# Two products fewer on TensorE, and a bias loaded ahead of its weight, in the opening of a conditioned feed-forward kernel

## What is computed

```python
q_emb = relu(cond @ W3 + b3)                       # one row of 512 per batch
h     = (64 * x + x.sum(axis=1, keepdims=True)) * q_emb[:, None, :]
h0    = relu(h @ W2 + b2)
y     = square(relu(h0 @ ternary(W_fc).T))
out   = x + rms_norm(y) @ ternary(W_proj).T
```

## Time and profile before

| | before |
|---|---|
| median of 3 executions | 312.59 us (312.39 to 313.21) |
| the profiled execution's own time | 312.75 us |
| its span, first to last instruction | 311.0 us |
| TensorE busy | 305.5 us, 98% |
| VectorE, ScalarE, GpSimd busy | 61%, 61%, 33% |

### The profile page before, as it was taken

The page is one execution under the profiler, slowest core; times in us unless marked ns, Lnnn a source line. Parts: engine busy times, 40 slices in busy tenths (PEclk is TensorE's granted clock), DMA queues, the critical chain, the costliest instruction groups (busy, mean ns, idle before and its releaser), DMA issues.

```text
span 311.0 us, 3798 instructions
## 1 busy us (share of the span) xinstructions
PE 305.5 (98%) x1286; PEld 233.7 (75%) x1286; DVE 188.7 (61%) x318; ACT 191.1 (61%) x282; POOL 102.0 (33%) x94
## 2 busy tenths in 40 slices
PE   8999999999999999999999999999999999999995
PEld 7764545446888888888888888888888888888883
DVE  0589999995778877888348235952223484222245
ACT  1685366696999699977646554445555445555540
POOL 1012333345433223344342431253333314333330
PEclk9999999999999999999999999999999999999999
DMA  6999435443464041115004300340000033000003
GB/s 211 354 274 277 173 73 99 133 112 93 125 212 103 1 102 37 34 34 52 17 0 147 125 0 1 133 140 0 0 2 0 0 135 137 0 0 0 2 2 136
DMA packets 31332, 27.03 MB, mean 87 GB/s; under 512 B 18736, under 2 KB 20816, under 8 KB 31312
## 3 DMA queue, kind: packets, MB, share of 16 engines
q1 hardware_dynamic: 29936, 26.22, 29.8%
q10 hardware_dynamic: 1376, 0.56, 0.7%
HBM read 18.39 MB, written 4.19 MB: 73 GB/s over the span
## 4 chain that ended last, share of the span: by engine, by line
PE 98%; DVE 0%; issue 0%; POOL 0%; POOLq 0%; DVEq 0%
PE ps_out L360 37%; PE ps_acc L348 37%; PE ps_acc L332 18%; PE ps_out L310 2%; PE ps_out L319 1%; PE ps_acc L404 1%; PE ps_x L419 1%; PE ps_acc L411 0%; PE ps_x L394 0%; DVE x_sb L565 0%; DVE x_t L495 0%; PE ps_x L400 0%; PE ps_acc L407 0%; POOL ident_f L712 0%; POOL ident_f L710 0%
## 5 line engine op out<-in xcount | busy, mean ns | idle before, releaser
L243 POOL TENSOR_TENSOR wv_sb<-wv_sb 128x512 f32<-128x512 f32 x55 | 71.7, 1304 | 122.7 <-DVE y_lo L510 115.6
L348 PE MATMUL ps_acc<-h_hi,w_t 128*128 128x512 f32 x256 | 100.0, 391 | 0.0
L360 PE MATMUL ps_out<-w_t,y_hi 128*128 128x512 f32 x256 | 100.0, 391 | 0.0
L360 PE MATMUL ps_out<-w_t,y_lo 128*128 128x512 f32 x256 | 99.6, 389 | 0.0
L348 PE MATMUL ps_acc<-h_lo,w_t 128*128 128x512 f32 x256 | 99.6, 389 | 0.0
L508 DVE CAST y_hi<-x_t 128x512 fp32r<-128x512 f32 x64 | 33.2, 518 | 86.9 <-PE ps_out L360 70.2
L655 ACT ACTIVATE x_t<-ps_acc 128x512 f32<-128x512 f32 x64 | 37.8, 591 | 61.1 <-PE ps_acc L348 61.1
L332 PE MATMUL ps_acc<-x_t,wv_sb 128*128 128x512 f32 x128 | 56.3, 593 | 0.3 <-DVE x_t L495 0.3
L348 PEld LDWEIGHTS ps_acc<-h_lo,w_t 128*128 128x128 f32 x256 | 48.1, 188 | 10.2 <-issue 0.2
L348 PEld LDWEIGHTS ps_acc<-h_hi,w_t 128*128 128x128 f32 x256 | 48.1, 188 | 10.2 <-issue 0.2
L360 PEld LDWEIGHTS ps_out<-w_t,y_hi 128*128 128x128 f32 x256 | 48.1, 188 | 9.9
(11 more groups left out here) (61 smaller groups left out, 163.6 us busy)
## 6 DMA issues: line engine op xcount, KB each, us to landing
x_sb<-in_x_dram SPq DMA_DIRECT2D x5, 1024.0 KB, 5.3
raw<-in_L_ffn_W_fc_dram SPq DMA_DIRECT2D x8, 512.0 KB, 7.0
raw<-in_L_ffn_W_proj_dram SPq DMA_DIRECT2D x8, 512.0 KB, 4.2
out_dram<-x_sb SPq DMA_DIRECT2D x16, 256.0 KB, 2.1
x_odd<-in_x_dram SPq DMA_DIRECT2D x2, 1024.0 KB, 7.6
x_sb<-in_x_dram SPq DMA_DIRECT2D x4, 256.0 KB, 4.2
wv_sb<-in_L_cond_W_dram SPq DMA_DIRECT2D x4, 256.0 KB, 8.7
x_t<-in_L_cond_W_dram ACTq DMA_DIRECT2D x1, 512.0 KB, 4.6
```

What stands on the lines that cost most here:

```text
L243: engine.tensor_tensor(acc, acc, y_sq[:, v % SQ_RING, :], ALU.add).then_inc(sq_added, 1)
L348: last = pe.matmul(ps_acc[:, (UNITS + v) % ACC_RING, :], w_t[:, j, k * P:(k + 1) * P], part[:, k, g * BANK:(g + 1) * BANK], start=(k == 0 ...
L360: last = pe.matmul(ps_out[:, t, :], part[:, v % RING, t * P:(t + 1) * P], w, start=(opens(v) and part is y_hi), stop=(closes(v) and part i ...
```

## The change

The two unread products between the turning of cond and the sums of x go. The load of `b_q` is issued ahead of that of `w_q` instead of behind it. Each bias has its own semaphore: the relu of q waits for `b_q` alone, and the wait for `b_v` stands behind the first `spread_pair`, ahead of the loop that holds `relu_h0`.

```diff
-        bias_loaded = sem("bias_loaded")
+        bq_loaded = sem("bq_loaded")
+        bv_loaded = sem("bv_loaded")
...
             last.then_inc(condt_done, 1)
-            for i in range(2):
-                pe.matmul(ps_acc[:, 1, 0:P], ident_f[:], ident_f[:], start=True, stop=True)
             pe.wait_ge(consts_ready, 1)
...
             act.dma_start(cond_sb, cond).then_inc(cond_loaded, 16)
+            act.dma_start(bq_t[:], b_q.rearrange("(m p) -> p m", p=P), allow_slow_non_contiguous=True).then_inc(bq_loaded, 16)
             act.dma_start(wq_sb[:], w_q.rearrange("(k p) d -> p k d", p=P)).then_inc(wq_loaded, 16)
-            act.dma_start(bq_t[:], b_q.rearrange("(m p) -> p m", p=P), allow_slow_non_contiguous=True).then_inc(bias_loaded, 16)
-            act.dma_start(bv_t[:], b_v.rearrange("(m p) -> p m", p=P), allow_slow_non_contiguous=True).then_inc(bias_loaded, 16)
+            act.dma_start(bv_t[:], b_v.rearrange("(m p) -> p m", p=P), allow_slow_non_contiguous=True).then_inc(bv_loaded, 16)
             act.wait_ge(consts_ready, 1)
             act.activation(root[:, 0:1], ones[:], ACT.Sqrt)
-            act.wait_ge(bias_loaded, 32)
+            act.wait_ge(bq_loaded, 16)
             act.wait_ge(q_done, 1)
...
             spread_pair(0)
+            act.wait_ge(bv_loaded, 16)
             for u in range(UNITS):
```

## The result

The changed kernel takes 315.76 us, median of 6 executions (314.94 to 317.25), against 312.49 us for the kernel before (6 executions, 311.87 to 313.21): a ratio of 1.0112, 95% interval 1.0091 to 1.0132. By the medians it is 3.3 us slower, by the ratio 3.5; that is outside the range, and the forecast was no change. The profiled execution took 317.25 us with a span of 315.4 us, 4.4 us more than the span before.

A forecast was written before the change was run, and what follows sets the result against it. TensorE bounds the kernel, and only the 10.5 us before `make_h0`'s first product can change: -0.45 (products), 0 (waits), +0.5 (w_q late) give +0.05, so 312.8 us (312.65 against the median); range 311.9 to 313.5.

The forecast's parts named there:

- What bounds the kernel, and where to look: TensorE bounds, busy 98% of the span; any effect must show in the first `make_h0` product's start, 12.08 us.
- The two products, 0.45 us: Before x's sums: four matrix instructions fewer save 0.45 us, with the clock's rise unmoved at 7.2 us.
- The waits, nothing: At the relu of q and behind `spread_pair(0)`: splitting the bias waits gives 0, as cover for the 0.45.
- b_q ahead of w_q: Loads before the query's products: w_q lands at 8.0 us, L419 starts at 8.1 instead of 7.6, 0.5 us lost.
- The bound above: w_q's latest landing, 8.4 us: 5.8 + 2.6, if b_q costs all that it cost in its old place.
- The sum: Start to first `make_h0` product: -0.45 (products), 0 (waits), +0.5 (w_q late), together +0.05 us.
- the clock rises late: Rival: x's tile 1 lands after 6.2 us, PE idles before the rise; 313.9 to 315.5 us, chance 0.07.
- a fall back to 421 ns behind the gap: Sign at PE's gap before the query products: slow instructions behind it would prove the sum wrong.
- w_q far too late: Rival: w_q lands from 8.9 us on, L419 at 9.0; +0.95, about 313.55 us, chance 0.07.

The follow-up runs named there:

- e1: Kernel before without the two unread products, loads and waits as before; 312.15 us, ratio 0.9984 to the kernel before.
- e3: Changed kernel with the two loads swapped back, w_q ahead of b_q; 312.25 us, ratio 0.9981 to the kernel before.
- e9: e3 with a second, contiguous copy of b_q (4 rows of 128 values) loaded ahead of w_q, relu of q waiting for it too; 314.62 us, ratio 1.0069.
- e4: e3 with the two unread products put back, so only the waits are split; 312.63 us, ratio 0.9992 to the kernel before.
- e12: e3 with ScalarE waiting for GpSimd's clearing before it issues w_q, at 1.69 us; 315.67 us, ratio 1.0090 to the kernel before.
- e7: Changed kernel with six unread products right in front of the wait for w_q; 313.78 us, ratio 1.0046 to the kernel before.
- e5: e1 with TensorE also waiting for the first block of w_v ahead of the query's products; 316.95 us, ratio 1.0119 to the kernel before.
- e11: Changed kernel with the query made behind x's tile 2; 313.07 us, ratio 1.0033 to the kernel before.
- e6: Kernel before, products kept, with TensorE also waiting for w_v's first block ahead of the query's products; 315.44 us, ratio 1.0102.
- e10: Changed kernel with two unread products right in front of the wait for w_q; 314.09 us, ratio 1.0056 to the kernel before.
- e13: e12 with the two biases issued only once w_q has landed; 321.38 us, ratio 1.0287 to the kernel before.
- e2: Changed kernel with the two unread products put back; 313.44 us, ratio 1.0029 to the kernel before.
- e14: e12 with SyncE waiting for GpSimd's clearing before it issues x's tile 2; 316.51 us, ratio 1.0113 to the kernel before.
- e15: Changed kernel with SyncE waiting for GpSimd's clearing before it issues x's tile 2; 315.00 us, ratio 1.0068 to the kernel before.

## Why the prediction was wrong

**What bounds the kernel, and where to look: right.** All of the loss is made before the first product of `make_h0`, or in that product's low clock; from 17.4 us on nothing differs.

**The two products, 0.45 us: right.** e1 gives 0.5 us with an interval of 0.1 to 0.9. The ground that I gave for it, that nothing moves the clock's rise, was not: it moves from execution to execution by itself. The first sixteen instructions of x's sums are the gauge:

```profile
4.31 3.63 PE L310 MATMUL ps_out<-sum_mat,x_sb 128*128 128x128 f32 x16
```
```profile
4.31 3.00 PE L311 MATMUL ps_out<-sum_mat,x_sb 128*128 128x128 f32 x16
```
```profile
4.30 2.46 PE L313 MATMUL ps_out<-sum_mat,x_sb 128*128 128x128 f32 x16
```

These are e1, e3 and e9, which are alike up to there. The Trainium skill (TensorE: Matmul & The Clock Gate, "What's actually happening") states this variation, and these rows bear it out; the 500 ns either way that it gives are less than what the traces show, where by the clock's records the rise came at 5.2 us in e9, 6.3 in e3 and 7.65 in e1. I had quoted the variation and then reckoned with one moment, 7.2 us.

**The waits, nothing: right.** e4 is at 0.9992.

**b_q ahead of w_q: the step that failed.** "I take the time of b_v less a little, 2.2 us: w_q lands at 8.0", with 5.8 and 8.4 as bounds. It landed at 9.6 in the changed kernel, 8.1 to 9.0 in the other kernels with the same order of loads and tile 2 in its place. The bound above was taken from what b_q cost behind w_q; what w_q itself loses by a later issue was not in any row before, and e12 shows that this alone takes it to 9.4. (A slip beside it: eight instructions of 0.21 us from 4.31 end at 6.0 and not at 6.2; nothing hangs on it, tile 1 landed at 5.3.) I read the rule of the Trainium skill (DMA: Bandwidth & Descriptors, "Rules for kernel authors") that strided values become one descriptor each as the reason against the edit. The rule agrees with the packets, 539 under 512 bytes between 3.5 and 5.25 us where e9 has 32, and they do slow the engines. But what I drew from it, that one contiguous piece would leave w_q near 5.8, is not borne out: e9 has four pieces there, and w_q landed at 9.0.

**The price of the gap: left out, and the larger half of the miss.** The sum charged the gap its own length, 0.5 us, and put what the gap does to the clock at nothing. The rival "the clock rises late" had the right mechanism's neighbour: it looked for a gap before the rise, at tile 1, which was in time. The gap behind the rise, at w_q, was in the forecast with 0.5 us and no word on the clock, though the last paragraph named "a fall back to 421 ns behind the gap" as what would prove the sum wrong. It did: some 2.0 us of the 3.3 (e7 against the change), and by itself, without any late load, the gap brought the clock down in 5 of 5 (e5).

**The chances.** "w_q far too late" (from 8.9 us on) is what happened; it had 0.07 and +0.95. The runs show +1.5 for it by itself (e7) and 3.3 with the clock.

## What to carry to other kernels

A load that has slack is still on the path if one that has none is put ahead of it, or if it is merely issued later: its landing doesn't shift by the delay, in the traces here 0.5 us of issue cost 2 to 4 us of landing. And a gap of TensorE near the start costs its length and then, perhaps, a stretch at half the clock worth more than the gap; so put needed work there first (e11), unneeded work second (e7), and never take a filler away in the same edit that makes the gap longer. Where two edits are meant to serve each other, measure each alone: here, by the medians, one won 0.6 us, one lost 0.7, and both lost 3.3.

## What was not expected of the hardware

- A gap as short as 0.85 us was followed by a fall of the granted clock, while one of 2.34 us was not. Gap and first work behind it in e6 and e10, then in e9, then e9's stretches:

```profile
9.51 2.00 PE L420 MATMUL ps_x<-h_f,x_t 128*128 128x32 f32 x16 [1.00 <-DMA wv_sb<-in_L_cond_W_dram]
11.32 3.65 PE L310 MATMUL ps_out<-sum_mat,x_sb 128*128 128x128 f32 x16
```
```profile
8.89 2.27 PE L420 MATMUL ps_x<-h_f,x_t 128*128 128x32 f32 x16 [0.85 <-DMA x_t<-in_L_cond_W_dram]
```
```profile
9.10 1.94 PE L420 MATMUL ps_x<-h_f,x_t 128*128 128x32 f32 x16 [2.34 <-DMA x_t<-in_L_cond_W_dram]
10.88 2.03 PE L313 MATMUL ps_out<-sum_mat,x_sb 128*128 128x128 f32 x16
```
```profile
9.10:13.00 3.90, 3.81 (x32) 1.00 1.09 341
13.20:20.00 6.80, 6.80 (x16) 1.00 1.07 368
```

  The length of the gap is not all. In the twelve traces with a gap ahead of the query's products, the moment at which the clock first rose goes with the fall better than the length does (us, from the traces' clock records; e13's first gap and fall):

| trace | first rise | gap | fall | back up |
|---|---|---|---|---|
| e2 | 5.0 | 7.1 to 8.2 | none | |
| e14 | 5.1 | 6.8 to 8.0 | none | |
| e9 | 5.2 | 6.8 to 9.1 | none | |
| e13 | 5.3 | 6.8 to 10.0 | 12.1 | 15.5 |
| e7 | 5.3 | 8.2 to 8.9 | none | |
| e12 | 5.5 | 6.9 to 9.5 | 8.9 | 15.7 |
| e15 | 5.7 | 7.0 to 9.2 | 9.1 | 15.9 |
| e11 | 6.2 | 8.1 to 9.1 | none | |
| e10 | 6.9 | 8.0 to 8.9 | 10.3 | 13.8 |
| the change | 7.1 | 7.7 to 9.7 | 10.5 | 17.4 |
| e5 | 7.2 | 7.7 to 9.5 | 10.6 | 17.4 |
| e6 | 7.9 | 8.5 to 9.5 | 11.3 | 14.7 |

  Of the five with a rise by 5.3 us only e13, with the longest gap, fell; of the seven with a later one all but e11 fell. This is one execution of each kernel, and no run sets the moment of the rise, so it is not shown as a cause; but it would explain why a single execution can go either way.
- The fall has two sizes. Three executions of the change took 314.94 to 315.00 us at a mean clock of 0.992 to 0.993, three 316.52 to 317.25 at 0.987 to 0.989; the table has low stretches of two lengths.
- The clock can fall after TensorE has worked again for a while (0.8 us in the changed kernel, 1.8 in e6) or while it still idles. In e12 it fell at 8.9 us, inside the gap that ended at 9.49:

```profile
6.95:8.85 1.90, 0.00 (x0) 1.00 0.76 205
8.95:9.45 0.50, 0.00 (x0) 0.50 1.04 239
```

  It then stays down through dense work. e13, with two long gaps, was at the lower level twice; stretches of e13, with all engines:

```profile
12.20:15.40 3.20, 3.01 (x15) 2.71 (x13) 0.00 (x0) 0.16 (x1) 0.00 (x0) 0.50 0.97 294
15.60:18.80 3.20, 0.00 (x0) 0.00 (x0) 0.00 (x0) 0.18 (x1) 0.00 (x0) 1.00 0.87 262
19.79:25.70 5.91, 5.91 (x7) 2.48 (x8) 5.67 (x10) 5.91 (x7) 0.00 (x0) 0.50 0.48 133
```

  In the middle stretch it is back at the upper level while TensorE does nothing at all.
- The granted clock reads 1.00 before the first rise too, when instructions take 421 ns; at the start of an execution only durations tell the level.
